# Identity matmuls on TensorE ahead of and inside an attention stage

## The chip, the cores and the metric

The kernel runs on one core of one Trainium2 chip. The metric is the device time of one execution in microseconds (us), taken as the median of the runs. The engines are named as in the profile: PE is TensorE, DVE is VectorE, ACT is ScalarE, POOL is GpSimd, SP is SyncE, which here only issues transfers.

## The reference

Two sequences (b = 0, 1) of 512 tokens with 128 features pass four residual blocks, all in float32. The change lies in the third, a cross-attention with 16 heads of 8 features over 154 context tokens:

```
x = x + L0_xattn(layernorm(x), ctx)        # elu-kernel attention, then a layernorm
x = x + L0_ffn(layernorm(x))               # gated recurrent cell, two steps
Q = (layernorm(x) @ Wq + bq)   16 heads of 8;   K, V = ctx @ Wkv + bkv
x = x + softmax(mask(Q K^T / sqrt(8))) V @ Wo + bo
x = x + top-2 of 8 experts (gate, W1, relu, W2) of layernorm(x)
```

## The kernel before

The program is written by hand, one instruction stream for each engine, with semaphores between them. Nothing is scheduled by a tool: the order within an engine is the order in the code. A matmul writes into one of eight PSUM banks, each of 128 partitions by 512 float32.

The stages before the third block end at L876, where TensorE multiplies the normed tokens by Wq, once for each sequence. DVE splits the result into three bf16 parts (L1265 to L1272) and SP issues DMAs (L448) that lay them out as `q_stack`: for each head, 48 rows of parts, a row for the mask, and three rows that later hold the row maximum. TensorE waits for this layout (`q_stacked[0]`) before it goes on.

Then the scores are made in groups of up to three heads by 128 queries (`scores`, L882: 49 rows by 154 columns, bf16). There are 24 groups for each sequence. The first 12, `END[0][0]`, run alone and rotate over four banks, `RING` = 0, 1, 6, 7. DVE takes the row maxima of each group (L1278). After the twelfth, DVE splits the maxima into bf16 parts (L1285 to L1288), TensorE turns them (`max_turn`, L891), ACT copies them out (L587) and a DMA (L453) puts them into `q_stack`.

After that TensorE runs 40 units, 20 for each sequence (`UPB` is 20). A unit u computes transposed scores less their maxima (`st(u)`, L924, 52 rows by 512 columns, or L928, four pieces of 32 output rows) into bank `RING[u % 4]`, ACT takes the exponential (L693), and four units later TensorE multiplies by the values (`pv`: after the fourth and the fifth unit of five, L948 and L951, float32). Between units stand the `items`: the remaining score groups and maxima turns, which alternate over banks 2 and 3. Seven items run before unit 0, then one or two after each unit. Output pieces of the first sequence (`tail`, L970 to L997) are woven into the second sequence's units, and the experts' matmuls (L1024 to L1046) follow.

`ident_b` is a 128x128 bf16 identity that POOL makes at the start. It serves to turn the maxima.

Of the kernel before, what the change touches and what calls it, by code (L numbers as in the profile page):

```python
# [20 lines left out]
P = 128  # L21
NB = 2
NJ = 4
# [65 lines left out]
def two_blocks(nc, x, ctxt, mask, w_ctx, w_l0, w_ffn, w_l1, cols, rows, w1, w2, b2, out):  # L89
    with ExitStack() as ctx:  # L90
        def sb(name, shape, dt=F32):
            return ctx.enter_context(nc.sbuf_tensor(name, shape, dt))

        bank = [ctx.enter_context(nc.psum_tensor(f"bank{i}", [P, 512], F32)) for i in range(8)]

        def sem(name):
            return ctx.enter_context(nc.semaphore(name))
# [25 lines left out]
        ident_b = sb("ident_b", [P, P], BF16)  # L123
# [71 lines left out]
        nmax = sb("nmax", [P, NB, NJ, H])  # L195
        nm_r1 = sb("nm_r1", [P, NB, NJ, H])
        nm_part = [sb(f"nm_part{k}", [P, NB, NJ, 3, n], BF16) for k, (_, n) in enumerate(HALVES)]
        nm_f = [sb(f"nm_f{k}", [3 * n, T], BF16) for k, (_, n) in enumerate(HALVES)]
        o_ev = ((q_m[:, 0], q_m[:, 1], q_e[:, 0], q_e[:, 1]), (a_f[:, 0], a_f[:, 1], cell[:, 0], cell[:, 1]))
        rsum = sb("rsum", [P, NB, HQ, NJ * HG])  # L200
# [117 lines left out]
        max_taken = sem("max_taken")  # L318
# [45 lines left out]
        UPB = H + HQ  # L364
        UNITS = [(hq, i) for hq in range(HQ) for i in range(HG + 1)]
        UNITS_ALL = NB * UPB
        RING = (0, 1, 6, 7)
# [8 lines left out]
        END = [[sum(v[:2] <= (b, k) for v in GROUPS) for k in range(2)] for b in range(NB)]  # L376
# [18 lines left out]
        def bank_of(n):  # L395

            return RING[n % 4] if n < END[0][0] else TB[ITEMS.index(n) % 2]
# [17 lines left out]
        def _(sp):  # L415
# [19 lines left out]
            for b in range(NB):  # L435

                for s, (_, kp) in enumerate(SLOTS):
                    sp.dma_start(k_stack[BP * b + HD * s:BP * b + HD * s + HD], k_part[:, b, kp])\
                      .then_inc(k_stacked[b], 16)
                sp.dma_start(k_stack[BP * b + ROW_MASK:BP * b + ROW_MASK + 1],  # L440
                             mask_b[0:1, b:b + 1, :].broadcast_to([1, H, TKP])).then_inc(k_stacked[b], 16)
# [335 lines left out]
        def _(pe):  # L777
# [16 lines left out]
            for b in range(NB):  # L794
# [14 lines left out]
                o = bank[4 + b][:, 0:P + 1]  # L809
# [22 lines left out]
            for g in range(3):  # L832
                last = pe.matmul(bank[1][:, g:g + 1], wf_s[:, (3 + g) * P:(4 + g) * P], col[:, C_INC:C_INC + 1],
                                 start=True, stop=True)
# [7 lines left out]
            for step in range(NB):  # L842
                pe.wait_ge(z_f_ready, step + 1)
                for g in range(3):
                    mm = pe.matmul(bank[3 * step + g][:], wf_s[:, g * P:(g + 1) * P], z_f[:, step],  # L845
                                   start=True, stop=step == 0)
# [24 lines left out]
            for b in range(NB):  # L871
# [3 lines left out]
                pe.wait_ge(s_f_ready, b + 1)  # L875
                pe.matmul(bank[4 + b][:], w3_s[:, 0:P], s_f[:, b], start=True, stop=True).then_inc(q1_mm, 1)  # L876

            def scores(n):

                b, _, j, h0, nh = GROUPS[n]  # L880
                for i in range(nh):
                    last = pe.matmul(bank[bank_of(n)][:, i * TK:(i + 1) * TK],  # L882
                                     q_stack[BP * b:BP * b + ROWS_SCORE, h0 + i, j * P:(j + 1) * P],
                                     k_stack[BP * b:BP * b + ROWS_SCORE, h0 + i, 0:TK], start=True, stop=True)
                last.then_inc(score_mm, 1)
# [8 lines left out]
            def item(i):  # L894
                if i >= 2:

                    before = ITEMS[i - 2]
                    if isinstance(before, tuple):
                        pe.wait_ge(nm_f_ready, 2 * before[0] + before[1] + 1)
                    else:  # L900
                        pe.wait_ge(max_taken, before + 1)
                it = ITEMS[i]
                if isinstance(it, tuple):
                    max_turn(*it)
                else:
                    if it == END[0][1]:
                        pe.wait_ge(q_stacked[1], 16 * (len(SLOTS) + 1))
                        pe.wait_ge(k_stacked[1], 16 * (len(SLOTS) + 2))
                    scores(it)

            def st(u):

                b, n = divmod(u, UPB)
                hq, i = UNITS[n]
                pe.wait_ge(nm_stacked[b][0], 16)
                if hq * HG + (i if i < HG else HG - 1) >= HALVES[1][0]:
                    pe.wait_ge(nm_stacked[b][1], 16)
                if u < 4:
                    pe.wait_ge(max_taken, END[0][0])
                else:  # L920
                    pe.wait_ge(prob_ready, u - 3)
                o = bank[RING[u % 4]]
                if i < HG:
                    last = pe.matmul(o[:], k_stack[BP * b:BP * b + ROWS_ALL, hq * HG + i, 0:P],  # L924
                                     q_stack[BP * b:BP * b + ROWS_ALL, hq * HG + i], start=True, stop=True)
                else:
                    for g in range(HG):
                        last = pe.matmul(o[KB * g:KB * g + KB], k_stack[BP * b:BP * b + ROWS_ALL, hq * HG + g, P:TKP],  # L928
                                         q_stack[BP * b:BP * b + ROWS_ALL, hq * HG + g], start=True, stop=True)
                last.then_inc(st_mm, 1)  # L930
# [118 lines left out]
            def y_turn(k):  # L1049
# [3 lines left out]
                    last = pe.transpose(bank[to][:, j * P:(j + 1) * P], y_f[:, b, j * P:(j + 1) * P], ident[:])  # L1053
                last.then_inc(y_tr, 1)

            pe.wait_ge(q_stacked[0], 16 * (len(SLOTS) + 1))
            pe.wait_ge(k_stacked[0], 16 * (len(SLOTS) + 2))
            pe.wait_ge(x2_ready, NB)
            for n in range(END[0][0]):
                if n >= 4:  # L1060
                    pe.wait_ge(max_taken, n - 3)
                scores(n)
            for u in range(-1, UNITS_ALL + LAG):
                if 0 <= u < UNITS_ALL:
                    st(u)
                if u == UNITS_ALL + 2:
                    up(0)
                if u >= LAG:
                    pv(u - LAG)
                if u < UNITS_ALL:  # L1070
                    for i in items_after(u):
                        item(i)
                if u - UPB in UNIT_PE:
                    tail(*UNIT_PE[u - UPB])
# [373 lines left out]
```

## Time and profile before

| | |
|---|---|
| median of 3 runs | 239.56 us (239.51 to 242.68) |
| the profiled execution | 237.72 us |
| its span, first to last instruction | 235.5 us |
| mean granted TensorE clock | 0.79 |
| PE busy | 170.0 us, 72% |
| DVE busy | 162.8 us, 69% |
| ACT busy | 100.9 us, 43% |
| POOL busy | 88.7 us, 38% |

The span leaves out 2.2 us around the program. Busy shares are means over stages; a PE row counts as busy until its modelled end. The granted clock is given as a share of full speed: 1.00 is 2.4 GHz, 0.50 is 1.2 GHz.

### The profile page before, as it was taken

The numbers are of one execution on the slowest core, as the hardware profiler recorded it, in microseconds if no ns is written. First come the engines' busy times: TensorE is split into PE (matmuls) and PEld (weight loads), VectorE is DVE, ScalarE is ACT, GpSimd is POOL, SyncE is SP. The second block draws the span as 40 slices with busy tenths as digits, with TensorE's granted clock in tenths as the row PEclk, the third lists the DMA queues.
The fourth block names the chain that finished last, engine by engine and source line by source line (L and its number), as shares of the span: only waits on it lengthen the run. The fifth ranks groups of instructions, "written<-read, shape, count | busy, mean of one in ns | idle before, by whom it ended". The sixth has DMA issues, their size and how long they took to land.

```text
span 235.5 us, 2445 instructions
## 1 busy us (share of the span) xinstructions
PE 170.0 (72%) x708; PEld 90.1 (38%) x708; DVE 162.8 (69%) x392; ACT 100.9 (43%) x183; POOL 88.7 (38%) x92
## 2 busy tenths in 40 slices
PE   0577740696737009478999899797898959999984
PEld 0333530342322007133323344334465736656652
DVE  5597999373377939744743622561699999999992
ACT  2138503333234000044525447545665664775751
POOL 3377024791079900000000000200397846966650
PEclk9999555599755555555755789979999997999999
DMA  6911200006001555100000000000000000001001
GB/s 208 327 33 28 57 1 0 0 1 177 1 1 31 68 78 77 17 4 6 0 0 5 3 4 0 0 0 3 0 1 0 1 0 3 0 0 45 0 3 45
DMA packets 6834, 7.23 MB, mean 31 GB/s; under 512 B 2318, under 2 KB 5798, under 8 KB 6822
## 3 DMA queue, kind: packets, MB, share of 16 engines
q1 hardware_dynamic: 5986, 5.60, 10.5%
q0 software_dynamic: 272, 1.05, 1.6%
q10 hardware_dynamic: 564, 0.43, 0.6%
q8 instruction: 6, 0.10, 0.2%
q14 instruction: 6, 0.05, 0.1%
HBM read 4.32 MB, written 0.52 MB: 21 GB/s over the span
## 4 chain that ended last, share of the span: by engine, by line
PE 39%; DVE 36%; DMA 9%; ACT 7%; issue 7%; SPq 1%; POOL 0%; ACTq 0%; DVEq 0%
DVE prob L1364 6%; DVE nmax L1278 5%; PE bank L948 5%; DMA q_stack<-prob 4%; PE bank L951 4%; DVE stats L1105 3%; PE bank L845 3%; PE bank L882 3%; DMA wc_s<-in_w_ctx 3%; DVE a_n L1116 3%; PE bank L924 2%; DVE q_m L1180 2%; PE bank L1044 2%; DVE hid_l L1374 2%; PE bank L780 2%
## 5 line engine op out<-in xcount | busy, mean ns | idle before, releaser
L564 POOL TENSOR_TENSOR hid_l<-prob,hid_h 128x512 fp32r<-128x512 f32 x27 | 42.2, 1576 | 34.6 <-DVE hid_h L1367 31.1
L481 POOL TENSOR_TENSOR rstd<-vare,m_half 128x4 f32<-128x4 f32 x10 | 11.4, 1137 | 99.9 <-DVE vare L1110 96.5
L1278 DVE TENSOR_REDUCE nmax<-bank 128x3 f32<-128x462 f32 (+1 forms) x48 | 25.8, 581 | 20.2 <-PE bank L882 19.9
L693 ACT ACTIVATE prob<-bank 128x512 f32<-128x512 f32 x40 | 23.4, 597 | 28.0 <-PE bank L924 17.8
L882 PE MATMUL bank<-k_stack,q_stack 49*128 49x154 bf16 x128 | 21.0, 306 | 17.2 <-DMA q_stack<-prob 12.5
L1364 DVE TENSOR_TENSOR prob<-prob,w_s 128x512 f32<-128x512 f32 x32 | 29.8, 945 | 1.0 <-ACT prob L735 0.5
L882 PEld LDWEIGHTS bank<-k_stack,q_stack 49*128 49x128 bf16 x128 | 12.2, 121 | 36.2 <-DMA q_stack<-prob 14.1
L735 ACT ACTIVATE prob<-bank,col 128x512 f32<-128x512 f32 x32 | 21.5, 692 | 4.9 <-PE bank L1026 4.8
L780 PE MATMUL bank<-ident,a_n 128*128 128x128 f32 x40 | 8.2, 342 | 16.2 <-DVE a_n L1116 16.2
L924 PE MATMUL bank<-q_stack,k_stack 52*128 52x512 bf16 x32 | 15.3, 492 | 2.1 <-DMA q_stack<-nm_f 2.1
L1044 PE MATMUL bank<-hid_h,w_h 128*128 128x512 f32 x32 | 14.1, 440 | 1.5 <-DVE hid_l L1374 1.4
L1024 PE MATMUL bank<-e_h,w_h 128*128 128x512 f32 x32 | 14.5, 454 | 0.0
L780 PEld LDWEIGHTS bank<-ident,a_n 128*128 128x128 f32 x40 | 5.9, 179 | 22.3 <-issue 18.3
L1367 DVE CAST hid_h<-prob 128x512 fp32r<-128x512 f32 x16 | 13.6, 850 | 0.6
L720 ACT ACTIVATE w_s<-bank 128x512 f32<-128x512 f32 x16 | 9.6, 598 | 9.1 <-PE bank L1008 9.0
L1046 PE MATMUL bank<-hid_l,w_h 128*128 128x512 f32 x32 | 13.1, 410 | 0.0
L741 ACT ACTIVATE hid_h<-prob 128x512 fp32r<-128x512 f32 x16 | 10.1, 628 | 7.0 <-DVE prob L1364 6.9
L1045 PE MATMUL bank<-hid_h,w_l 128*128 128x512 f32 x32 | 13.1, 408 | 0.0
L948 PE MATMUL bank<-prob,v_a 128*32 128x512 f32 x64 | 12.7, 881 | 0.0
L587 ACT ACTIVATE nm_f<-bank 27x512 bf16<-27x512 bf16 (+1 forms) x4 | 2.3, 584 | 24.3 <-PE bank L891 24.3
L1026 PE MATMUL bank<-e_h,w_l 128*128 128x512 f32 x32 | 12.7, 397 | 0.0
L1025 PE MATMUL bank<-e_l,w_h 128*128 128x512 f32 x32 | 12.6, 394 | 0.0
(202 smaller groups left out, 331.0 us busy)
## 6 DMA issues: line engine op xcount, KB each, us to landing
q_stack<-prob SPq DMA_DIRECT2D x12, 128.0 KB
w_s<-in_w SPq DMA_DIRECT2D x1, 1024.0 KB, 8.7
w_s<-in_w POOLq DMA_DIRECT2D x1, 1024.0 KB, 6.9
x_t<-in_x SPq DMA_DIRECT2D x2, 256.0 KB, 3.2
wf_s<-in_w_ffn SPq DMA_DIRECT2D x1, 512.0 KB, 7.8
k_stack<-prob SPq DMA_DIRECT2D x12, 40.0 KB
row<-in_rows SPq DMA_DIRECT2D x1, 452.0 KB, 7.0
wc_s<-in_w_ctx ACTq DMA_DIRECT2D x1, 256.0 KB, 6.9
```

The source lines that it names most:

```text
L564: pool.tensor_tensor(hid_l[:, g % NH], hid[:, g % NH], hid_h[:, g % NH].bitcast(F32), ALU.subtract).then_inc(hid_lo_pool, 1)
L693: nc.scalar.activation(prob[:, u % NPR], bank[RING[u % 4]][:], ACT.Exp).then_inc(prob_ready, 1)
L735: nc.scalar.activation(hid[:, g % NH], bank[RING[g % 4]][:], ACT.Relu, bias=col[:, C_B1 + v:C_B1 + v + 1], scale=1.0).then_inc(hid_full, 1)
L780: last = pe.transpose(dst[:, j * P:(j + 1) * P], src[:, j], ident[:])
L882: last = pe.matmul(bank[bank_of(n)][:, i * TK:(i + 1) * TK], q_stack[BP * b:BP * b + ROWS_SCORE, h0 + i, j * P:(j + 1) * P], k_stack[BP * ...
L924: last = pe.matmul(o[:], k_stack[BP * b:BP * b + ROWS_ALL, hq * HG + i, 0:P], q_stack[BP * b:BP * b + ROWS_ALL, hq * HG + i], start=True, ...
L948: last = pe.matmul(o[GW * g:GW * g + GW], v_a[:, b, hq * HG + g], prob[:, (u - i + g) % NPR], start=True, stop=False)
L1024: pe.matmul(o, wh, e_h[:, b], start=True, stop=False)
L1044: pe.matmul(y, w2_h[:, e, c], hh, start=False, stop=False)
L1278: dve.tensor_reduce(nmax[:, b, j, h0:h0 + nh], src.rearrange("p (h k) -> p h k", k=TK), AX.X, ALU.max, negate=True).then_inc(max_taken, 1)
L1364: dve.tensor_tensor(h, h, comb_b[:, n % NCB], ALU.mult).then_inc(weighted, 1)
L1367: dve.tensor_copy(hid_h[:, g % NH], h).then_inc(hid_hi[0], 1)
```

## The change

A new helper `stream(n, b)` issues n matmuls of `ident_b` by `ident_b` repeated four times, 128 rows by 512 columns in bf16, into bank b. Their results are not read: each is overwritten by the next matmul that the kernel itself makes into that bank. No wait is added or removed, and no other engine's instructions change. The helper is called at four places: 56 times ahead of the wait for `q_stacked[0]`, once ahead of each of the first 12 score groups, 8 times ahead of unit 0 (before its wait for the maxima in `q_stack`), and once ahead of every even unit of the first sequence.

```diff
+            def stream(n, b):
+                for _ in range(n):
+                    pe.matmul(bank[b][:].rearrange("p (r c) -> p r c", c=P), ident_b[:],
+                              ident_b[:].rearrange("p (o c) -> p o c", o=1).broadcast_to([P, NJ, P]),
+                              start=True, stop=True)
...
             def scores(n):
                 b, _, j, h0, nh = GROUPS[n]
+                if n < END[0][0]:
+                    stream(1, bank_of(n))
...
                 hq, i = UNITS[n]
+                if u == 0:
+                    pe.wait_ge(max_taken, END[0][0])
+                    stream(8, RING[0])
                 pe.wait_ge(nm_stacked[b][0], 16)
...
                     pe.wait_ge(prob_ready, u - 3)
+                if u < UPB and u % 2 == 0:
+                    stream(1, RING[u % 4])
                 o = bank[RING[u % 4]]
...
+            stream(56, RING[0])
             pe.wait_ge(q_stacked[0], 16 * (len(SLOTS) + 1))
```

On TensorE, the wait for the query stack in the changed kernel (L881 is the new matmul, L876 the query projection, L891 here the scores):

```order
L876 MATMUL bank5<-a_f,w3_s 128x512 [waits s_f_ready]
L881 MATMUL bank0<-ident_b 128x512 x56
L881 MATMUL bank0<-ident_b 128x512 [waits x2_ready,k_stacked0,q_stacked0]
L891 MATMUL bank0<-k_stack,q_stack 128x154 x3
L881 MATMUL bank1<-ident_b 128x512
L891 MATMUL bank1<-k_stack,q_stack 128x154 x3
```

The 56 stand before the wait and can run in it; the one that waits belongs to the first score group.

On TensorE, around unit 0 in the kernel before (L882 scores, L924 the unit's own matmul):

```order
L882 MATMUL bank3<-k_stack,q_stack 128x154 x2
L882 MATMUL bank2<-k_stack,q_stack 128x154 [waits max_taken]
L924 MATMUL bank0<-q_stack,k_stack 128x512 [waits max_taken,nm_stacked0_0]
L882 MATMUL bank3<-k_stack,q_stack 128x154 [waits max_taken]
L882 MATMUL bank3<-k_stack,q_stack 128x154 x2
```

The same place in the changed kernel (L891 scores, L938 the unit's own matmul):

```order
L891 MATMUL bank2<-k_stack,q_stack 128x154 [waits max_taken]
L881 MATMUL bank0<-ident_b 128x512 [waits max_taken]
L881 MATMUL bank0<-ident_b 128x512 x7
L881 MATMUL bank0<-ident_b 128x512 [waits max_taken,nm_stacked0_0]
L938 MATMUL bank0<-q_stack,k_stack 128x512
L891 MATMUL bank3<-k_stack,q_stack 128x154 [waits max_taken]
```

Eight new matmuls stand ahead of the wait for the maxima's transfer and a ninth behind it.

## Rows read from the trace of the kernel before

**Rows 1.** The page: busy PE tenths and granted clock in 40 slices of the span.

```profile
PE   0577740696737009478999899797898959999984
PEclk9999555599755555555755789979999997999999
```

**Rows 2.** Windows of the span: busy us (instructions) by engine, clock, DMA share, GB/s.

```profile
55.10:58.50 3.40, 1.30 (x4) 0.24 (x2) 2.00 (x3) 1.69 (x3) 0.00 (x0) 1.00 0.93 273
58.50:61.90 3.40, 3.17 (x4) 1.36 (x5) 0.08 (x1) 0.69 (x1) 0.00 (x0) 0.50 0.07 20
61.90:65.30 3.40, 1.46 (x9) 0.78 (x7) 2.39 (x12) 0.69 (x1) 0.18 (x1) 1.00 0.00 0
...
75.50:88.00 12.50, 0.01 (x1) 0.00 (x0) 9.04 (x9) 0.00 (x0) 6.74 (x8) 0.50 0.57 73
...
94.50:99.50 5.00, 2.21 (x12) 1.05 (x12) 3.73 (x11) 0.59 (x1) 0.00 (x0) 0.50 0.10 16
...
101.50:109.50 8.00, 7.18 (x38) 3.43 (x38) 5.49 (x13) 4.52 (x8) 0.00 (x0) 0.50 0.00 0
...
113.10:116.50 3.40, 2.96 (x23) 0.98 (x21) 2.43 (x6) 2.02 (x4) 0.00 (x0) 1.00 0.00 0
116.50:125.80 9.30, 8.72 (x42) 2.90 (x42) 4.73 (x12) 3.77 (x8) 0.00 (x0) 0.50 0.00 0
125.80:130.20 4.40, 4.40 (x16) 1.08 (x15) 1.60 (x3) 1.19 (x2) 0.00 (x0) 0.50 0.02 6
130.20:133.60 3.40, 2.44 (x20) 1.28 (x20) 2.59 (x7) 2.07 (x4) 0.00 (x0) 1.00 0.00 0
133.60:137.00 3.40, 3.40 (x18) 1.06 (x16) 0.98 (x5) 0.60 (x1) 0.00 (x0) 0.50 0.02 5
137.00:150.70 13.70, 12.61 (x69) 5.35 (x69) 5.51 (x24) 8.18 (x15) 1.22 (x2) 1.00 0.01 2
...
101.50:134.20 32.70, 29.90 (x155) 11.28 (x155) 18.39 (x42) 14.90 (x27) 0.00 (x0) 0.60 0.01 2
```

**Rows 3.** Timeline of PE and DVE, 73 to 96 us.

```profile
73.44 2.07 PE L876 MATMUL bank<-a_f,w_s 128*128 128x512 f32 x2 [0.69 <-ACT a_f L587]
...
88.03 6.46 PE L882 MATMUL bank<-k_stack,q_stack 49*128 49x154 bf16 x42 [12.51 <-DMA q_stack<-prob]
88.63 6.64 DVE L1278 TENSOR_REDUCE nmax<-bank 128x3 f32<-128x462 f32 x12 [3.88 <-PE bank L882]
```

**Rows 4.** The chain that ended last, 98 to 103 us: start, us, what.

```profile
98.64 2.84 DMA q_stack<-nm_f
...
102.14 0.39 PE bank L882 x3
102.52 0.43 PE bank L924
```

**Rows 5.** Timeline of PE at clock 0.50, units 0, 12 and 17 and a value product.

```profile
101.53 0.61 PE L924 MATMUL bank<-q_stack,k_stack 52*128 52x512 bf16 x1 [2.06 <-DMA q_stack<-nm_f]
...
116.67 0.58 PE L924 MATMUL bank<-q_stack,k_stack 52*128 52x512 bf16 x1
...
125.33 0.58 PE L924 MATMUL bank<-q_stack,k_stack 52*128 52x512 bf16 x1
...
125.84 1.93 PE L948 MATMUL bank<-prob,v_a 128*32 128x512 f32 x8
...
128.33 2.03 PE L951 MATMUL bank<-prob,v_b 128*128 128x512 f32 x2
```

**Rows 6.** Timeline of PE at clock 1.00.

```profile
140.96 0.60 PE L924 MATMUL bank<-q_stack,k_stack 52*128 52x512 bf16 x2
...
147.30 1.06 PE L948 MATMUL bank<-prob,v_a 128*32 128x512 f32 x8
148.30 0.39 PE L924 MATMUL bank<-q_stack,k_stack 52*128 52x512 bf16 x1
148.62 1.13 PE L951 MATMUL bank<-prob,v_b 128*128 128x512 f32 x2
```

## Prediction, made before the changed kernel was run

> **What bounds the kernel now.** I read the page first, for where TensorE is busy and at which clock. In [rows 1] PE goes from nothing to nine tenths busy between slices 13 and 17 (76 to 100 us) and stays there, while the granted clock is 5 tenths in nearly all slices from 11 to 22. The attention stage thus runs its matmuls at 1.2 GHz. The windows, read second, put times to it. From 65.3 us on the clock is at 0.50, but for two short stretches, until 137.0 [rows 2]. Between 101.5 and 134.2 us, where the first sequence's units run, PE is busy 29.90 of 32.70 us at a mean clock of 0.60, DVE 18.39 and ACT 14.90. PE sets the pace there, and a faster PE clock would show.
>
> The timeline, third, tells what lies ahead of that. L876 ends at 73.44 + 2.07 = 75.51 us and the scores start at 88.03, after 12.51 us idle behind the DMA of the query stack [rows 3]. The first 12 score groups then take 6.64 us on DVE, 0.55 each, and DVE is the pace: PE waits for it once four banks are full. The chain, fourth, goes over the transfer of the maxima, 2.84 us from 98.64 [rows 4]; PE stands idle for 2.06 us before unit 0 at 101.53 [rows 5].
>
> What moves the clock, as the windows show it: 3.17 us busy of 3.40 with full-array 128x512 float32 matmuls (58.5 to 61.9) came before a rise; 1.46 and 1.30 us busy of 3.40 came before falls [rows 2]. But 8.72 us busy of 9.30 (116.5 to 125.8) did not bring a rise, and 2.96 of 3.40 (113.1 to 116.5) came before a fall. In those two stretches much of PE's work is 49x154 scores and 52x512 units, which use less than half of the array's rows, or L948 with 32 output columns of 128. So I read it that full-array work counts, and narrow work counts less. The new matmuls are full-array, 128 rows by 128 columns.
>
> The Trainium skill (TensorE: Matmul & The Clock Gate, "What's actually happening") says that the clock is throttled by default and that activity of PE releases it. By its plain sense of busy or idle the stage from 101.5 us would have been at full clock already, with 29.90 of 32.70 us busy, and the streams inside the units would only cost. The windows speak against that plain reading, and the sum goes by them.
>
> **The change part by part.** A 512-column matmul behind another costs 0.43 us at clock 0.50 [rows 4]. At 1.00 two together take 0.60 and one 0.39, so 0.21 us more [rows 6].
>
> *56 matmuls in the wait.* PE is idle there anyway, and nothing else uses bank 0. All at 0.21 they take 11.8 us of the 12.51 and cost nothing. All at 0.43 they take 24.1, end at 99.6 us instead of 88.03, and cost 11.6. Between these ends the moment of the rise decides. I take the 3.4 us of the stretch from 58.5 to 61.9 [rows 2], counted from 75.5: 8 of them at 0.43 us until 78.9, then 48 at 0.21, end at 89.0, cost **+1.0**. If L876 already counts, the rise is at 76.9 and the cost is 0.
>
> *One ahead of each of 12 score groups.* At 1.00 a group is 0.21 and half of the three scores' 0.39 [rows 4], 0.41 against DVE's 0.55: hidden by DVE, **0**. If the clock were at 0.50, 0.43 + 0.39 - 0.55 = 0.27 for each, 3.2 in all.
>
> *Eight ahead of unit 0, and a ninth.* Their cover is the 2.06 us idle behind the maxima's transfer. At 1.00 the eight take 1.7 and fit, and the ninth, behind the wait, costs 0.2. At 0.50 they take 3.4, come 1.4 late, and the ninth adds 0.4: 1.8. From 94.5 to 99.5 us PE has only 2.21 us busy of 5.00, less than in the stretches before the falls, and narrow work at that. I take the clock to have dropped by then: **+1.8**. Queued behind the late unit 0 are the items that DVE waits for, so the lateness passes on.
>
> *Nine more ahead of units 2 to 18.* They stand on PE, the pacing engine. At 0.21 they cost 1.9 us, at 0.43 3.9. With a fifth of them slow: **+2.3**.
>
> *The clock in the units.* At 0.50, units 12 to 17 take 125.33 - 116.67 = 8.66 us for five [rows 5]. In them L948 and L951 take 1.93 + 2.03 = 3.96, against 1.06 + 1.13 = 2.19 at 1.00 [rows 6]: 1.8 saved. The other 4.7 us of PE would save 2.35 if it halved, and nothing if DVE took over, which has 4.73 us of work in 9.30 there [rows 2]. The two hand groups back and forth over two banks, so I take the middle, 1.1. That makes 2.9 of 8.66, or 0.33 us saved for each us turned to full clock. Between 101.5 and 137.0 the slow stretches add up to 8.0 + 3.6 + 9.3 + 4.4 + 3.4 = 28.7 us. All turned: 9.5. The streams keep full-array work inside the gaps between value products, which is where the clock fell at 116.5, but the thin start of the stage and units 19 on have few of them. I take four fifths turned: **-7.6**. The ends are none turned, 0, and all, -9.5.
>
> What is late next is DVE with its maxima and ACT with its exponentials. The batch after 137.0 ran at 1.00 already for 13.7 us [rows 2] and gains nothing; it and the experts only move forward. No DMA and no other engine's instruction is added.
>
> Sum: 1.0 + 0 + 1.8 + 2.3 - 7.6 = -2.5, which makes 235.2 of the profiled execution's 237.72 us. The median of the runs, 239.56, stands 1.84 above that execution, and all three runs lie above it: when the clock rose by itself in the units (twice, 3.4 us each) was luck of the execution. A program that holds the clock leans less on it, and I put 0.5 us on that: 239.56 - 2.5 - 0.5 = **236.6 us**.
>
> **The rivals.**
>
> *All of it works.* The rise comes with L876's help (0), the eight streams run fast (0.2), the nine as well (1.9), and all slow stretches turn (-9.5): -7.4, 232.2 us. For it: DVE and ACT have room. Against: the thin work from 94.5 to 101.5, which no stream covers before 99.5.
>
> *Half of it is lost.* The clock drops at the maxima's transfer, the 52x512 units and their streams before the first value product don't bring it back (in 101.5 to 109.5, 7.18 us busy of 8.00 did not), and it flickers afterwards. A third turned is -3.2, against 1.0 + 1.8 and 3.1 for the nine streams, mostly slow: +2.7, 242.3 us. For it: the clock in the trace fell twice in the midst of the units.
>
> *Slower: identity matmuls don't release the clock.* Their data are almost all zeros, and no row shows such work at either clock but the narrow turn of the maxima. Then the 56 last until 99.6 us (+11.6), the 12 pace the first scores (+3.2), the nine before unit 0 are late (+1.8), and the rest cost 3.9: +20.5, 260 us. It needs no full failure: with n of the 56 at 0.43 us the end is 75.5 + 11.8 + 0.22 n, and it passes 2% on the wrong side from n = 25, a rise 11 us after L876's end. Against it: the same engine rises after 3.4 us of other full-array work.
>
> *The change doesn't do what it says*, in that the stage isn't bound by PE: then full clock in the units saves only part. Its price lies in the 0 to 2.35 from which I took 1.1, and it is inside the first and second cases.
>
> **How the numbers follow.** Forecast, 60 to 90% of the slow stretches turned: 0.50, about 235 to 239 us. All works: 0.20. Half lost: 0.22. Not released: 0.06. Rest 0.02. A difference under 2%, 4.8 us, can't be told from none in this kernel, so faster means under 234.8. That takes nearly all of the second case and the edge of the forecast: 0.25. Slower means over 244.4: the 0.06 and a part of the third case's spread, 0.09. The same: 0.66. The range reaches from 232.5, amid the second case, to 242.3, the third case's value, and leaves out about 0.2.
>
> **What the profile would show.** The clock in windows from 78 to 94 us should be 1.00, the stream's end 88 to 90, and the scores start right behind it. DVE should still take the 12 groups in 6.6 us. A 0.50 near 99 us and a unit 0 at 103 to 105 would confirm the third term. Five units should take near 6.3 us with their streams, at 1.00. I am wrong if the clock in the stream stays at 0.50 beyond 82 us, if the units stay at 0.50 for over half of their time, or if they run at 1.00 and five still take 8 us because DVE or the handing back and forth holds them.

## The result, and the profile after

The changed kernel took 249.39 us (median of 4 runs, 248.57 to 253.05), the kernel before 239.53 us in the same comparison. The ratio is 1.0432, with a 95% interval of 1.0337 to 1.0527: slower by 4.3%, where 236.6 us was forecast. The profiled execution took 248.57 us with a span of 246.4. Ratios here are of the runs within 1.5% of the fastest of their kernel and medians are of all runs, so a kernel whose runs scatter, as the kernel before with 235.15 to 245.83 us over all comparisons, stands lower in a ratio than by its median. No other engine's instructions changed, so the trace can be laid beside that of before. TensorE did get one wait more, against what the section on the change says: the diff's `wait_ge` on the row maxima ahead of the eight, for a value that unit 0 waits for anyway.

The windows of the changed kernel (columns as in [rows 2]):

```profile
65.90:79.50 13.60, 9.60 (x21) 4.12 (x22) 10.84 (x22) 4.91 (x10) 12.20 (x14) 0.50 0.18 24
79.50:100.00 20.50, 18.59 (x103) 8.27 (x101) 14.88 (x23) 0.00 (x0) 3.47 (x3) 1.00 0.56 61
100.00:106.80 6.80, 5.37 (x20) 2.17 (x20) 1.87 (x5) 0.59 (x1) 0.00 (x0) 0.50 0.04 7
106.80:110.20 3.40, 2.77 (x20) 1.43 (x19) 2.17 (x5) 2.05 (x4) 0.00 (x0) 0.99 0.00 0
110.20:130.70 20.50, 19.79 (x82) 6.32 (x82) 9.47 (x22) 6.88 (x13) 0.00 (x0) 0.50 0.01 2
130.70:134.10 3.40, 3.11 (x23) 1.27 (x22) 2.05 (x4) 1.94 (x5) 0.00 (x0) 1.00 0.00 0
134.10:147.80 13.70, 13.06 (x54) 4.51 (x54) 5.37 (x14) 4.63 (x9) 0.00 (x0) 0.50 0.01 2
107.00:145.20 38.20, 35.93 (x165) 12.76 (x164) 18.51 (x42) 14.90 (x27) 0.00 (x0) 0.59 0.01 2
```

The stream in the wait raised the clock to 1.00 at 79.5 us and the first scores kept it until 100.0. But from unit 0 at 107.0 to unit 22 at 145.2 the mean clock is 0.59, against 0.60 before [rows 2]: two short stretches at full clock, as before, and 38.2 us where 32.7 were. DVE has the same 18.5 us of work.

The timeline of PE and DVE in the changed kernel (start, us, engine, line; L881 is the identity matmul, L891 the scores, L938 a unit, L1293 the maxima), which answers to [rows 3, 5]:

```profile
75.79 14.50 PE L881 MATMUL bank<-ident_b 128*128 128x512 bf16 x57
90.22 0.37 PE L891 MATMUL bank<-k_stack,q_stack 49*128 49x154 bf16 x3
...
90.63 7.51 DVE L1293 TENSOR_REDUCE nmax<-bank 128x3 f32<-128x462 f32 x12 [5.38 <-PE bank L891]
...
103.15 3.92 PE L881 MATMUL bank<-ident_b 128*128 128x512 bf16 x9
107.00 0.39 PE L938 MATMUL bank<-q_stack,k_stack 52*128 52x512 bf16 x1
...
126.04 0.60 PE L938 MATMUL bank<-q_stack,k_stack 52*128 52x512 bf16 x1
...
134.34 0.58 PE L938 MATMUL bank<-q_stack,k_stack 52*128 52x512 bf16 x1
```

The 56 and the first group's own end by 90.2 us, and the groups follow. DVE takes 7.51 us for twelve groups, not 6.64. The nine before unit 0 take 3.9 us. Units 12 and 17 are the second and third L938 rows: five units take 8.3 us.

The chain of the changed kernel (start, us, what) shows two things that [rows 4] did not:

```profile
86.56 15.30 DMA q_stack<-prob
101.87 0.02 issue
101.89 0.59 ACT nm_f L587
102.48 0.05 issue
102.53 0.69 PE bank L891 x4
103.22 3.85 PE bank L881 x9
107.07 0.32 PE bank L938
...
113.25 0.54 PE bank L881
113.79 0.54 PE bank L938
```

ACT's copy of the maxima is released by the second sequence's query stack, which it waits for in its program order, and that lands at 101.87 us only; TensorE's turn of the maxima was done a microsecond earlier. And an identity matmul between other work costs 0.54 us of the chain at clock 0.50, not 0.43.

### The profile page after: what moved, and what is told of

Its sections match the earlier page's. It is cut to its first block, busy times and chain, and to the rows that moved or that the text cites. A ratio compares the mean times of both kernels' runs of the same rounds, so it can differ in the third digit from the quotient of the medians.

```text
span 246.4 us, 2617 instructions
## 1 busy us (share of the span) xinstructions
PE 195.3 (79%) x794; PEld 98.3 (40%) x794; DVE 163.7 (66%) x392; ACT 100.8 (41%) x183; POOL 88.7 (36%) x92
## 4 chain that ended last, share of the span: by engine, by line
PE 42%; DVE 33%; DMA 9%; ACT 7%; issue 6%; SPq 1%; POOL 0%; ACTq 0%; DVEq 0%
DMA q_stack<-prob 6%; DVE prob L1379 5%; PE bank L962 5%; PE bank L965 4%; PE bank L891 4%; DVE stats L1120 3%; PE bank L881 3%; PE bank L845 3%; DMA wc_s<-in_w_ctx 3%; PE bank L938 3%; DVE a_n L1131 3%; DVE prob L1282 2%; DVE q_m L1195 2%; PE bank L1058 2%; PE bank L780 2%
## 5 line engine op out<-in xcount | busy, mean ns | idle before, releaser
L1293 DVE TENSOR_REDUCE nmax<-bank 128x3 f32<-128x462 f32 (+1 forms) x48 | 26.7, 583 | 29.5 <-PE bank L891 29.0
L881 PE MATMUL bank<-ident_b 128*128 128x512 bf16 x86 | 27.5, 448 | 0.0
L891 PE MATMUL bank<-k_stack,q_stack 49*128 49x154 bf16 x128 | 19.1, 275 | 4.7 <-DVE nmax L1293 2.8
L891 PEld LDWEIGHTS bank<-k_stack,q_stack 49*128 49x128 bf16 x128 | 10.3, 108 | 21.7 <-issue 13.9
L881 PEld LDWEIGHTS bank<-ident_b 128*128 128x128 bf16 x86 | 9.3, 109 | 14.6 <-issue 7.0
L938 PE MATMUL bank<-q_stack,k_stack 52*128 52x512 bf16 x32 | 14.7, 482 | 0.0
```

The source lines that it names most:

```text
L881: pe.matmul(bank[b][:].rearrange("p (r c) -> p r c", c=P), ident_b[:], ident_b[:].rearrange("p (o c) -> p o c", o=1).broadcast_to([P, NJ, P]),
L891: last = pe.matmul(bank[bank_of(n)][:, i * TK:(i + 1) * TK], q_stack[BP * b:BP * b + ROWS_SCORE, h0 + i, j * P:(j + 1) * P], k_stack[BP * ...
L1293: dve.tensor_reduce(nmax[:, b, j, h0:h0 + nh], src.rearrange("p (h k) -> p h k", k=TK), AX.X, ALU.max, negate=True).then_inc(max_taken, 1)
```

## The experiments

**The parts by themselves.** My first theory was that the stream slows the transfers (A), with chance as its rival (B), and that the units' identity matmuls only cost their time (C). Each of the four calls of `stream` was kept alone.

```diff
+            stream(56, RING[0])                     # only this
```


> Only the 56 identity matmuls in the wait for the query stack are kept. Theory A (the stream slows the transfers of the query stack): the stack's twelve DMAs move about 61 GB/s instead of 76, the first part lands 1.4 us later, the second part near 101 us instead of before 96, and ACT's copy of the maxima, which stands behind a wait for it, is released by that DMA. Then +3 to +3.5 us against the kernel before, with unit 0 at about 105. Theory B (the transfer's rate varied by chance, only the stream's own length counts): the DMA is done before 96, unit 0 at 102.5 to 103, +1 us.

Measured: 242.30 us median against 240.56; ratio 1.0243 (1.0111 to 1.0375). It is slower, by how much is unclear. Unit 0 started at 101.57 us, in a program that had reached the wait 4 us earlier than the changed kernel had. Its transfer moved 62 GB/s. Counted from the first issue of the query stack's transfers (70.71 us), unit 0 came after 30.9 us; with only the ten in the units, the first matmul behind the same wait came after 31.4 us (72.03 to 103.44), without any stream in between, and in the two profiles of the kernel before after 28.1 and 30.5. So the stream itself shows no cost here.

```diff
+                if n < END[0][0]:
+                    stream(1, bank_of(n))           # only this
```


> Only the one identity matmul ahead of each of the first 12 score groups is kept. Nothing raises the clock before them at first, so a group costs PE 0.43 + 0.39 us against DVE's 0.55: +0.27 a group, +3.2 us, if they stay at 0.50; if their full-array work raises the clock midway, +1.5 to +2. A theory by which added work on an engine that waits is free gives 0.

Measured: 244.48 us against 240.56; ratio 1.0349 (1.0143 to 1.0554), unclear in size but on the slower side of 1. The clock stayed at 0.50 through the twelve groups. That the medians differ by 3.9, near the 3.2, is luck: in the profile a group took 1.03 us (0.54 + 0.49 of the chain) and not 0.82, the twelve cost 5.9, and unit 0 started at 107.98 us instead of 101.53. Units 0 to 22 then took 28.8 us instead of 32.7, at a mean clock of 0.74, although no identity matmul stands among them.

```diff
+                if u == 0:
+                    pe.wait_ge(max_taken, END[0][0])
+                    stream(8, RING[0])              # only this
```


> Only the eight identity matmuls ahead of unit 0 are kept (not the ninth, which belongs to the even units). At clock 0.50 they take 3.4 us against 2.06 us of wait: unit 0 comes 1.4 us late and the kernel takes +1.4 us. If they raise the clock for the units behind them, up to 1.5 us of it comes back: 0. The theory that the maxima's transfer is slowed by them too would give over +2.

Measured: 238.42 us against 240.56 over 10 and 14 runs; ratio 1.0074 (0.9993 to 1.0155). That is no difference that can be told, though units 0 to 22 took 29.0 us at a mean clock of 0.74 in its profile, against 32.7 at 0.60, and 28.2 at 0.80 in a second one.

```diff
+                if u < UPB and u % 2 == 0:
+                    stream(1, RING[u % 4])          # only this
```


> Only the ten identity matmuls ahead of the even units of the first sequence are kept. Theory C (PE paces the units, the identity work does not hold the clock, and each costs its own time): ten at 0.43 to 0.54 us, +4 to +5.5 us, with the clock at 1.00 for no more than 7 us of the first sequence's units. The theory of the prediction (they hold the clock once a value product has raised it): the clock is at 1.00 in over half of the units and the kernel is -2 to -5 us.

Measured: 247.60 us against 240.56; ratio 1.045 (1.0318 to 1.0583). This call alone gives 7.0 us in these four runs, most of the changed kernel's 9.9; a fifth run, below, took 240.63. In its profile no stretch of the units ran at full clock (columns of [rows 2]; the first row lies in the transfer, the second is the units):

```profile
78.00:88.00 10.00, 0.01 (x1) 0.01 (x1) 5.29 (x5) 0.00 (x0) 3.11 (x3) 0.50 0.57 62
...
104.00:144.50 40.50, 39.29 (x165) 13.94 (x164) 18.78 (x42) 15.13 (x27) 0.00 (x0) 0.50 0.01 2
```

The transfer runs at 62 GB/s with PE idle beside it. So theory A is not needed for 62.

**The complement.** The changed kernel without its units' calls:

```diff
-                if u < UPB and u % 2 == 0:
-                    stream(1, RING[u % 4])
```


> The changed kernel without the identity matmuls ahead of the even units; those in the wait, the first scores and the eight stay. If the units' identity matmuls cost their own time (theory C), this is about 5 us faster than the changed kernel: +5 us against the kernel before. If they bought back part of it by the clock, taking them out changes the time by less than 2 us: +8 to +10.

Measured: 241.83 us, against 240.16 for the kernel before beside it. That is +1.7, where the changed kernel had +9.9. Units 0 to 22 took 31.7 us instead of 38.2. Both ways of looking put most of the loss on the ten matmuls in the units.

**What moves the clock.** The same 56 in the wait, first over 32 rows, then with 32 output columns:

```diff
-    pe.matmul(bank[b][:]..., ident_b[:], ident_b[:]...)
+    pe.matmul(bank[b][:]..., ident_b[0:32], ident_b[0:32]...)         # 32 rows
```


> Only the 56 matmuls in the wait, but of 32 rows by 128 columns of the identity (a quarter of the array's rows and a quarter of the partitions read). Theory A by the reads of SBUF: the DMAs keep more of their 76 GB/s, and the time is between the kernel before and the run with 128 rows. Clock: if the number of rows in use counts, it stays at 0.50, the 56 take 24 us, end near 99.6 and the kernel is +10 to +12 us; if any matmul counts as busy, it rises after about 3.5 us and the time is +0 to +3.


```diff
-    pe.matmul(bank[b][:]..., ident_b[:], ident_b[:]...)
+    pe.matmul(bank[b][0:32]..., ident_b[:, 0:32], ident_b[:]...)      # 32 columns
```


> Only the 56 matmuls in the wait, but with 32 output columns of the array instead of 128 (all 128 rows are read, the moving data are the same). Clock: if the columns in use count, it stays at 0.50, the 56 end near 99.6 and the kernel is +10 to +12 us; if not, it rises and the time is that of the full 56. DMA: if the reads of the moving data slow it, it is as slow as with the full 56; if the power or the writes into PSUM do, it is faster.

Measured: 241.90 and 242.13 us against 240.16. The times tell little, the windows a lot. Both programs were at 1.00 when the stream began, at 72.5 and 70.5 us. With 32 rows:

```profile
71.50:78.20 6.70, 6.70 (x29) 2.72 (x30) 6.60 (x5) 1.92 (x4) 6.41 (x8) 1.00 0.47 59
78.20:88.20 10.00, 10.00 (x25) 3.36 (x23) 4.41 (x5) 0.00 (x0) 2.22 (x2) 0.50 0.57 63
```

With 32 columns:

```profile
69.00:82.50 13.50, 13.05 (x58) 5.65 (x58) 11.53 (x10) 2.47 (x5) 9.12 (x10) 1.00 0.50 58
```

PE is busy without a gap in both streams. With 32 rows the clock fell in the midst of it and stayed at 0.50; with 32 columns it stayed at 1.00 to the stream's end at 82.8. Between these two executions, one of each, the clock went with the rows of the array in use and not with the output columns. That speaks against my reading that L948's 32 columns count for little, and for my reading that work over 49 rows, as the scores, or 52, as the units, does.

**More of it in the units.** Two ahead of every unit:

```diff
-                if u < UPB and u % 2 == 0:
-                    stream(1, RING[u % 4])
+                if u < UPB:
+                    stream(2, RING[u % 4])
```


> The changed kernel with two identity matmuls ahead of every unit of the first sequence instead of one ahead of every second, 40 instead of 10. Theory D (enough full-array work holds the clock): 1.00 from unit 1 to unit 19 but for a few us. Each pair then costs 0.43 to 0.54 us of PE at 1.00, 9 to 11 us in all, against the 4 to 5 us of the ten slow ones, and the units' own PE work halves: -3 to +2 us against the changed kernel. If the clock still flickers, each pair costs up to 0.97 us and the kernel is +10 us or more against the changed one.

Measured: 240.85 us (236.06 to 243.12), against 240.16: +0.7 where the changed kernel had +9.9, with 30 matmuls more. The window over units 0 to 22:

```profile
106.90:138.70 31.80, 30.86 (x194) 10.99 (x193) 18.12 (x42) 15.24 (x27) 0.00 (x0) 1.00 0.01 2
```

The clock holds, and 40 extra matmuls at full clock fit into less time than ten at half. Without the calls ahead of the units but for the eight:

```diff
-            stream(56, RING[0])
-                    stream(1, bank_of(n))           # and 1, or 2, ahead of every unit
```


> Eight identity matmuls ahead of unit 0 and one ahead of every unit of the first sequence; none in the wait for the query stack and none in the first scores. 20 in the units are between the 10 that did not hold the clock and the 40 that did. If 20 hold it: about 0.32 us each, 6.4 us, units 0 to 22 in 27 to 28 us, and with unit 0 1.4 us late the kernel is -3 us. If not, 20 times 0.43 to 0.54 us: +8 to +10.

> The same with two ahead of every unit. They held the clock in the run with 40, whose units 0 to 22 took 31.6 us against 32.6 before. Without the 56 and the twelve, unit 0 comes 1.4 us late instead of 5.5: the kernel is 0 to -1 us.

Measured: 250.75 us (single runs from 239.86 to 255.74) with one each, 242.17 (237.00 to 243.49) with two, against 240.88. One each is on the edge: its profiled execution held the clock (mean 0.96, units 0 to 22 in 30.0 us) and took 239.86 us, and the other runs took up to 16 us more. Those have no trace, but the mean clock of each is on record: 0.854 and 0.829 in the runs of 239.86 and 241.35 us, 0.801 in those of 250.47 and 251.02, 0.764 and 0.760 in those of 255.74 and 254.29. The slow ones had less of the full clock; where in the kernel they lost it isn't shown.

**Ten that bring little.** The units' ten over 32 rows:

> Only the ten identity matmuls ahead of the even units, but over 32 rows of the array. They cost PE the same time as those of 128 rows. Theory C: the time of the run with ten full ones, +7 us, or up to 2 us more, since they bring less toward a rise. If the full ones had bought back time by the clock, this is slower than them by over 3 us.

Measured: 246.00 us against 240.88; ratio 1.0216 (1.009 to 1.0342). The profile shows 40.4 us for units 0 to 22 at 0.50, the same as the 40.5 of the full ones. In these two profiles the full ones bought nothing back.

**Rows instead of time.** If it is rows that hold the clock, the units' own matmuls can use more of them. The keys lie in two tensors, one for each sequence, whose other rows are zeros, and the queries of both sequences already share the 128 partitions:

```diff
-   q_stack[BP * b:BP * b + ROWS_SCORE, ...], k_stack[BP * b:BP * b + ROWS_SCORE, ...]
+   q_stack[rows_of_n, ...], k_pad[b][rows_of_n, ...]      # 0:113 or 0:116, from unit 0 on
-   k_stack[BP * b:BP * b + ROWS_ALL, ...], q_stack[BP * b:BP * b + ROWS_ALL, ...]
+   k_pad[b][full, ...], q_stack[full, ...]                # 0:113 for b = 0, 0:116 for b = 1
+   sp.dma_start(q_stack[lo:hi], zeros_b...)               # rows 49:64 and 113:116
```


> The kernel before, with no identity matmul at all. The units of both sequences and the score groups from unit 0 on run over 113 or 116 rows of the array instead of 52 and 49; the added rows of the keys are zeros, so that the sums don't change. The matmuls keep their columns. Theory E (the clock follows the rows in use, and a row more costs no time): the clock stays at 1.00 from the first value product to the end of the first sequence's units, units 0 to 22 take 22 to 26 us instead of 32.6, and the kernel is -6 to -10 us. Rival (it follows the time in which PE is busy, or the columns): the clock is at 1.00 for 7 us as before and the time is within 1 us.

Measured: 229.37 us (228.20 to 232.91) against 240.88; ratio **0.9545** (0.9452 to 0.9638). Nothing of the computation is left out. The windows before and after the rise, and beyond:

```profile
101.30:113.00 11.70, 11.34 (x54) 5.33 (x55) 6.44 (x15) 5.39 (x10) 0.00 (x0) 0.50 0.01 2
113.00:128.70 15.70, 13.68 (x101) 6.06 (x100) 11.34 (x27) 9.59 (x18) 0.00 (x0) 1.00 0.01 3
101.30:128.70 27.40, 25.02 (x154) 11.39 (x155) 17.78 (x41) 14.98 (x27) 0.00 (x0) 0.79 0.01 2
113.00:184.60 71.60, 62.08 (x354) 33.83 (x352) 49.13 (x146) 44.22 (x81) 20.98 (x16) 1.00 0.01 2
```

Once risen at 113.0 us, behind the first value product, the clock does not fall for 71.6 us; in the kernel before it fell at 116.5, 133.6 and 154.1 us. The timeline rows of its units 12 and 17 (L938 over 113 rows) are the price at full clock:

```profile
116.70 0.38 PE L938 MATMUL bank<-q_stack,k_pad 113*128 113x512 bf16 x1
...
122.54 0.38 PE L938 MATMUL bank<-q_stack,k_pad 113*128 113x512 bf16 x1
```

Five units take 5.84 us, against 8.66 at 0.50 [rows 5], and one L938 takes 0.38 us over 113 rows, 0.39 over 52 [rows 6]. Of the 8.5 us between the spans of the two profiles (227.0 and 235.5), 5.3 lie in units 0 to 22 and 3.0 behind them.

Then the same with the eight ahead of unit 0, to raise the clock for the units before the first value product:

```diff
+                if u == 0:
+                    pe.wait_ge(max_taken, END[0][0])
+                    stream(8, RING[0])
```


> The run with 113 rows, and the eight identity matmuls ahead of unit 0. Theory E: they raise the clock behind unit 0, the units' own rows hold it, and the first eight units, at 0.50 until 113 us without them, run at 1.00. Gained 2 to 3 us there, lost 1.4 by the late unit 0: -1 to -2 us against the run with 113 rows alone. Rival: those first units are paced by the handing back and forth with DVE and ACT, the eight only cost their lateness: +1 to +1.5 us.

Measured: 230.05 us (226.09 to 231.90) against 240.05; ratio 0.9587 (0.9433 to 0.9741). Its profile has units 0 to 22 in 24.6 us at a mean clock of 0.95, as theory E wants, and its lowest run is the lowest of all. But the medians of the two don't differ by more than either spreads.

**The transfer's rate.** All ten profiles with the 56 or with matmuls in the units had it at 60 to 62 GB/s from 78 to 88 us, the kernel before and the runs with only the twelve, only the eight and only the 113 rows at 73 to 77. But the run with 113 rows and the eight, which has neither the 56 nor matmuls in the units, had 62. Three programs were profiled a second time, unchanged.

> The kernel before, profiled a second time. If the transfer's rate belongs to the program: 73 GB/s again in 78 to 88 us. If it belongs to the execution: 62 is as likely.

> The kernel with only the ten in the units, profiled a second time. Program: 62 GB/s again. Execution: 73 to 77 is as likely.

> The kernel with only the eight, profiled a second time. Program: 77 GB/s again. Execution: 62 is as likely.

Measured, the kernel before again (243.99 us), its transfer and its units 0 to 22:

```profile
78.00:88.00 10.00, 0.00 (x0) 0.00 (x0) 7.05 (x6) 0.00 (x0) 4.90 (x5) 0.50 0.57 60
...
104.30:137.20 32.90, 30.12 (x155) 11.39 (x155) 18.44 (x42) 15.11 (x27) 0.00 (x0) 0.60 0.01 2
```

It shows 60 GB/s, and unit 0 at 104.3 us instead of 101.5. Its chain holds the same wait as that of the changed kernel:

```profile
86.50 14.30 DMA q_stack<-prob
...
100.82 0.60 ACT nm_f L587
...
101.43 2.86 DMA q_stack<-nm_f
```

So one program runs at either rate, and the low one needs no stream: theory A isn't needed. The last transfer of the stack, too, was under way for 14.6 to 15.4 us in the slow profiles with the 56 where it shows on the chain, and for 14.3 to 15.2 us in those without. Theory B, chance alone, isn't proven by that: all eleven profiles with the 56 or with matmuls in the units ran at the low rate and two of the seven others, and no run says why.

The eight again had 75 GB/s (238.85 us). The ten in the units again had 62, and 240.63 us, on another chip than the 247.07 to 249.35 of the four runs: this time the clock rose at 126.9 us and stayed, and the second stretch is that of the units after it:

```profile
103.70:126.90 23.20, 22.49 (x100) 8.01 (x99) 10.42 (x21) 8.54 (x15) 0.00 (x0) 0.50 0.01 2
126.90:138.40 11.50, 10.15 (x67) 4.09 (x66) 7.73 (x21) 6.36 (x12) 0.00 (x0) 1.00 0.01 2
```

It doesn't show that the ten keep a full clock that has come. The eight alone, with nothing in the units, had such a stretch as well (0.99 from 121.2 to 131.7 us), and the changed kernel lost the clock twice after 3.4 us with the ten in it. Nor is it the forecast: units 0 to 22 took 34.7 us, against 32.7 and 32.9 in the two profiles of the kernel before.

## Why the prediction was wrong

*What bounds the stage* was right: PE at half clock sets the pace. With wider rows the same work of units 0 to 22 takes 27.4 us instead of 32.7, and 24.6 with the eight as well.

*The 56 in the wait*, +1.0: right in mechanism. The rise came at 79.5 us, 3.7 after the stream's start (3.4 taken), each cost 0.43 and then 0.22 us, and the scores began at 90.2 (89.0 forecast). But the second profile of the kernel before began them at 89.8 without any stream, so the stream itself cost nearly nothing there.

*One ahead of each score group*, 0: off by 0.9 us on DVE, whose twelve groups took 7.51 us instead of 6.64. PE became the pace at 0.62 us a group (0.32 + 0.31), where I had added 0.21 and half of 0.39: between two kinds of matmul each costs more than behind an equal one. Why, no run shows. The 0.9 didn't reach the chain, since ACT's copy of the maxima waited longer for the query stack.

*The nine before unit 0*, +1.8: right. They took 3.9 us at 0.50, and unit 0 started 4.6 us after the end of ACT's copy, against 2.9 in the second profile of before: 1.7 late. The clock had dropped at 100.0.

*Nine more in the units*, +2.3: too small. Six of them ran at half clock, at 0.54 us each, and three at 0.32: 4.2.

*The clock in the units*, -7.6: **this is the step that failed.** "I take four fifths turned" was none turned; the stretches at 1.00 add up to 6.8 us as before. I had seen that narrow work does not hold the clock, but had taken the ten for enough without setting them against anything: ten 512-column matmuls in 33 us are 2.2 us of full-clock work. The price of a turned us, 0.33 saved, was right: five units at full clock take 5.84 us (over 113 rows) against 8.66, where I had 5.8.

Summed in the profiled executions: unit 0 is 5.5 us later than in the first profile of before and 2.7 later than in the second, which had the same rate of transfer. So 2.8 of it is the luck of that first profile. Of the 2.7, the nine before unit 0 are 1.7, and 1.0 is the query stack's last transfer, under way for 15.30 us against 14.30; with no stream in the wait it took up to 15.21. Units 0 to 22 take 5.5 us more, 4.2 by the nine's own time and 1.3 unassigned. After unit 22 the two need 101.2 and 101.3 us. Between profiled executions the forecast was -2.5 us and the measured difference is +10.9. Of these 13.4 us, 7.6 are the turned clock that didn't come, 1.9 the nine in the units, 2.7 a unit 0 that came 5.5 us late where I had 2.8, and 1.3 unassigned, less 0.1 behind unit 22.

The third rival, "half of it is lost", had the right mechanism: the clock drops at the transfer of the maxima and flickers in the units. It still let a third be turned, which was none, and priced the streams at 0.43 at most. The one of the other side, that identity matmuls don't release the clock, was wrong: the clock rose 3.7 us into a stream of data that are nearly all zeros, while in the kernel before, with PE idle there, it stayed at 0.50.

The plain reading of the Trainium skill (TensorE: Matmul & The Clock Gate, "What's actually happening"), that activity of PE releases the clock, was rightly set aside: in the run with 32 rows PE was busy for 10.00 of 10.00 us at 0.50. The same page's advice to keep PE busy without gaps ("Why this matters for your kernels") would not have led to the remedy found here, as PE was busy for 29.90 of 32.70 us before.

## What to carry to other kernels

When the clock of PE falls though PE is busy, look at how many rows of the array its matmuls use before adding work to warm it. Zero rows added to the kernel's own matmuls cost them no time that the profile shows and the clock held (0.9545), while extra matmuls between them cost 0.32 to 0.54 us each and helped only where there were so many that the gain was spent. And ask of a warming measure whether it suffices at the slow clock, where each of its pieces takes twice as long; a half measure can be worse than none (10: 249.4 us, 40: 240.9, none: 240.2). A single execution doesn't tell it: with the same ten, one run took 240.63 us and four took 247.07 to 249.35.

## What the runs showed of the hardware

- With 56 matmuls of 128 rows by 32 columns the clock stayed at 1.00 for the 12 us that they took; with 32 rows by 128 columns it fell to 0.50 after 5.7 us of them, PE busy all the time. Each was traced once. Units and scores widened from 52 and 49 to 113 or 116 rows ran at 1.00 for 71.6 us on end.
- The same transfer of 128 KB pieces into the query stack ran at 60 to 62 GB/s in some executions and 73 to 77 in others, the kernel before at 73 and at 60. Between these two, unit 0 moved by 2.8 us. What sets it is open.
- A 512-column bf16 matmul of the identity behind an equal one costs 0.43 or 0.22 us by the clock; ahead of scores or a unit it costs 0.54 or 0.32 on the chain.
- One program had runs 16 us apart (239.86 to 255.74 us with one matmul for each unit), with mean clocks from 0.854 down to 0.760, so such a kernel needs many runs to be judged.
